# Zeroing a scratch table in seventeen pieces from the sync queue during the walk, and a neighbour comparison moved between the keys, in a graph network kernel

## What is computed

```
edge_index = jnp.stack([src, dst])
h = jnp.maximum(_layernorm(x, axis=-1), 0.0)
x = x + _L0_gnn_ref(h, edge_index, ...)
h = jnp.maximum(_layernorm(x, axis=-1), 0.0)
x = x + _L1_gnn_ref(h, edge_attr_8, edge_attr_64, edge_weight, ..., src, dst)
h = jnp.maximum(_layernorm(x, axis=-1), 0.0)
x = x + _L2_gnn_ref(h, ..., src, dst)
h = jnp.maximum(_layernorm(x, axis=-1), 0.0)
x = x + _L3_gnn_ref(h, L3_gnn_attn_w, src, dst)
```

## Time and profile before

| | us |
|---|---|
| median of 3 runs | 5092.41 (5090.03 to 5094.08) |
| profiled execution, its own time | 5095.59 |
| its span in the profile | 5093.8 |
| busy in the span: PE / DVE / ACT / POOL | 3575.9 / 4055.2 / 2002.8 / 1387.6 |

### The profile page before, as it was taken

One profiled execution on the slowest core, in us unless ns is written; L12 is line 12 of the kernel. 1 busy time (PEld: TensorE's weight loads), 2 busy tenths in 40 slices (PEclk: granted clock), 3 DMA queues, 4 the chain that ended last, 5 costly groups with the idle time before them and its releaser, 6 DMA issues. The chain is left out here.

```text
span 5093.8 us, 64935 instructions
## 1 busy us (share of the span) xinstructions
PE 3575.9 (70%) x19959; PEld 1591.3 (31%) x19959; DVE 4055.2 (80%) x7913; ACT 2002.8 (39%) x3932; POOL 1387.6 (27%) x2065
## 2 busy tenths in 40 slices
PE   3555551025608999999999359999999998147156
PEld 1111111001104555545555124444444443112122
DVE  4999994368866777777777789999999998588798
ACT  2888870046503333333333123333333332046065
POOL 0000006700055555555555112222222222100000
PEclk8999995567758999999999679999999999579579
DMA  6333338975433444444444113333333332345444
GB/s 265 137 137 140 142 137 275 363 228 186 138 122 102 112 112 112 111 111 111 111 112 112 32 53 87 90 88 89 89 88 90 87 90 73 123 153 201 150 157 172
DMA packets 347749, 673.72 MB, mean 132 GB/s; under 512 B 69724, under 2 KB 250396, under 8 KB 334864
## 3 DMA queue, kind: packets, MB, share of 16 engines
q1 hardware_dynamic: 305280, 564.32, 34.4%
q0 software_dynamic: 39680, 78.78, 5.9%
q10 hardware_dynamic: 2448, 26.48, 1.2%
HBM read 398.85 MB, written 270.50 MB: 131 GB/s over the span
## 5 line engine op out<-in xcount | busy, mean ns | idle before, releaser
L659 POOL DMA_INDIRECT arena<-h_table,gidx x808 | 763.4, 945 | 545.0 <-DVE gidx L1575 339.2
L792 PE MATMUL banks<-arena,lw 128*65 128x512 f32 (+3 forms) x1050 | 460.8, 595 | 298.6 <-DVE lw L1485 172.1
L1712 DVE TENSOR_TENSOR arena<-banks,arena 128x512 f32<-128x512 f32 x808 | 519.4, 684 | 110.9 <-PE banks L933 102.9
L741 PE MATMUL banks<-arena 128*128 128x500 bf16 x1440 | 365.6, 375 | 302.0 <-ACT arena L1079 293.5
L1587 DVE TENSOR_TENSOR arena<-banks,arena 128x512 f32<-128x512 f32 x808 | 535.1, 683 | 26.3 <-PE banks L838 0.6
L1719 DVE TENSOR_TENSOR arena<-banks,arena 128x512 f32<-128x512 f32 x808 | 536.1, 685 | 0.2 <-PE banks L938 0.2
L684 POOL TENSOR_TENSOR arena<-arena 128x72 f32<-128x72 f32 (+1 forms) x808 | 216.4, 299 | 984.3 <-DMA arena<-xs_dump 984.1
L1327 DVE TENSOR_SCALAR arena<-arena 128x500 bf16<-128x500 f16 x1440 | 440.7, 445 | 0.2 <-issue 0.2
L844 PE MATMUL banks<-arena 128*64 128x256 f32 x3232 | 438.6, 392 | 0.0
L949 PE MATMUL banks<-arena 128*64 128x256 f32 x3232 | 437.9, 392 | 0.5 <-DVE arena L1721 0.5
L938 PE MATMUL banks<-arena 64*128 64x512 f32 x1616 | 435.3, 616 | 0.8 <-DVE arena L1719 0.8
(11 more groups left out here) (281 smaller groups left out, 6446.1 us busy)
## 6 DMA issues: line engine op xcount, KB each, us to landing
arena<-c_flat SPq DMA_DIRECT2D x75, 1562.5 KB, 7.0
slots<-arena SPq DMA_DIRECT2D x90, 1000.0 KB, 3.9
arena<-hs_dump SPq DMA_DIRECT2D x404, 128.0 KB
arena<-mask_rows SPq DMA_DIRECT2D x50, 781.2 KB, 4.3
arena<-in_edge_attr SPq DMA_DIRECT2D x202, 128.0 KB
arena<-placed SPq DMA_DIRECT2D x202, 128.0 KB
xs_dump<-arena SPq DMA_DIRECT2D x202, 128.0 KB
hs_dump<-arena SPq DMA_DIRECT2D x202, 128.0 KB, 2.4
```

Source lines behind the costliest of these rows:

```text
L659: pool.indirect_dma_start(out=xs[par][:, k * D:(k + 1) * D], out_offset=None, in_=h_table, in_offset=bass.IndirectOffsetOnAxis(ap=gidx[par ...
L741: last = pe.matmul(ps[4 + r % 2][:, 0:BW], row_hot[r][:, k * P:(k + 1) * P], col_hot[r][:, k * BW:(k + 1) * BW], start=k == 0, stop=k == K ...
L792: last = pe.matmul(ps[j][0:rows, 0:n], lw[par][:, 0:rows], ptile[par][:, j * COLS:j * COLS + n], start=isinstance(b, int) and b == 0, stop ...
L1712: V.tensor_tensor(dt_[j % 2], ps[3 + j % 2][:, :], xat[q], ALU.mult).then_inc(dt_sb, 1)
```

## The change

The seventeen writes of zeros leave ScalarE's queue. SP issues one of them after every second `flush`, the first after eight steps of the walk. The tile, the sizes and the semaphore stay. The comparison's four lines move behind VectorE's four reads `offset` and ahead of its four reads `col_key`. Below the edit, line numbers in the changed kernel differ by a few.

```diff
@@ -421,6 +421,10 @@
             for i in range(SL // 8):
                 for par in range(2):
                     flush(i * 2 + par, par)
+                lo = i * CROW
+                if lo < W * D:
+                    n = min(CROW, W * D - lo)
+                    sp.dma_start(placed_v[:, lo:lo + n], zeros[:, 0:n]).then_inc(placed_zeroed, 16)
 
             for i in range(-(-WN // WIDE)):
                 n = min(WIDE * WD, N - i * WIDE * WD)
@@ -1058,11 +1062,6 @@
                     n = min(COLS, N - j * COLS)
                     act.activation(ot[0:rows, j * COLS:j * COLS + n], ps[j][0:rows, 0:n], ACT.Copy).then_inc(ot_sb, 1)
 
-            act.wait_ge(setup_d, 2)
-            for lo in range(0, W * D, CROW):
-                n = min(CROW, W * D - lo)
-                act.dma_start(placed_v[:, lo:lo + n], zeros[:, 0:n]).then_inc(placed_zeroed, 16)
-
             act.wait_ge(left_go, 1)
 
             def distance(s, r):
@@ -1287,10 +1286,6 @@
             dve.wait_ge(consts, 16)
             ran(V.tensor_scalar(row0, nid[:, 0:1], float(SL), None, ALU.mult))
             ran(V.tensor_copy(out=sel[:, :, :], in_=cst[:, C_SEL:C_SEL + 4 * P].rearrange("p (j m) -> p j m", j=4)))
-            dve.wait_ge(loaded, 16 * 6)
-            ran(V.tensor_tensor(same_prev[:, :], dsti[:, :], dprev, ALU.is_equal))
-            ran(V.tensor_tensor(same_next[:, :], dsti[:, :], dnext, ALU.is_equal))
-            ran(V.tensor_copy(out=firstc[:, 0:1], in_=dsti[:, 0:1]))
             settle()
 
             dve.wait_ge(key_ps, 1)
@@ -1300,6 +1295,10 @@
             for k in range(KE):
                 dve.wait_ge(key_ps, 2 + k)
                 V.tensor_tensor(offset[:, k, :], ps[k][:, 0:SL], base20, ALU.subtract).then_inc(key_sb, 1)
+            dve.wait_ge(loaded, 16 * 6)
+            ran(V.tensor_tensor(same_prev[:, :], dsti[:, :], dprev, ALU.is_equal))
+            ran(V.tensor_tensor(same_next[:, :], dsti[:, :], dnext, ALU.is_equal))
+            ran(V.tensor_copy(out=firstc[:, 0:1], in_=dsti[:, 0:1]))
             for k in range(KE):
                 dve.wait_ge(key_ps, 6 + k)
                 ran(V.tensor_tensor(col_key[:, k, :], ps[4 + k][:, 0:SL], base20, ALU.subtract))
```

## The result

| | before | after |
|---|---|---|
| median, us | 5091.98 (5090.03 to 5094.08, 4 runs) | 5030.05 (5030.02 to 5030.63, 4 runs) |
| profiled execution, its own time | 5095.59 | 5030.07 |
| its span | 5093.8 | 5028.3 |

The changed kernel is 61.9 us faster. The ratio of their times is 0.9879, with a 95% interval of 0.9861 to 0.9896.

The account below looks back on a forecast made before the run. DVE's two long early waits, for the walk's loads and for `x`, both behind the zeros, were taken as the bound. 25.8 + 29.3 = 55.1 us off 5092.4 gave 5037.3 us, range 5030 to 5050.

Parts of the forecast that it names:

- R1: Start: no tail on two engines, loads drain at full rate; 7 us more gained, 5030.3 us in all; chance 0.07.
- Part (a): Start: walk's loads without the zeros; DVE's first mask at 13.5 us, not 39.33; worth 25.8 us.
- the pairs with zero packets: Start, before the change: on one engine, load packets alternate with large zero packets, 0.41 us a pair; 72 pairs take 30 us.
- The sign of some 24 packets per microsecond: Start, new profile: about 24 DMA packets per microsecond should go on until DVE's first mask at 13 to 15 us.
- R2: Start: scattered single numbers, not zeros, make the loads late; DVE still starts at 39.33; 5063.1 us; chance 0.05.
- Part (b): From DVE's first mask to the walk's first step: 29.8 us instead of 59.1; worth 29.3 us.
- The lower clock: TensorE's selections before the walk: a lower granted clock in the second half of their run would cost 0.7 us.
- Part (c): Before the walk: `loaded` is there at 28 us, needed by 30.9 to 31.8; hidden, about 4 us to spare.
- the 40 packets at 0.18 us: Late engine after 13 us: five loads of 8 rows ahead of `x`, 7.3 us in all.
- R3: Comparison's new place: `x` ends the wait, rows cost 0.083 us each, `loaded` near 44 us; 5049 us; chance 0.07.
- Part (d): In the walk: zeros between flushes cost nothing; a piece ends 6.2 us after its issue, next flush issued after 7.4.
- R4: Walk's shared queue: pieces over 8.4 us each stop DVE 17 times; at 13 us each, 78 us, so 5115; chance 0.03.

## Why the prediction was right

**The number.** 5037.3 us was forecast and 5030.05 measured. The range's lower bound of 5030 was taken from R1, whose 5030.3 is nearly what was measured, though its condition (no tail on two engines) did not hold: it needed the first mask at about 6.5 us, and it came at 13.38. That the result fell inside the range and not just outside is luck. That DVE's first step would come 55 us earlier, and for which reasons, is not; the later 5034.45 also lies within the narrower 5034 to 5046. (The bounds given for the terms and the spread add up to 5034 and 5049, not 5046.)

**The reading of the start held.** Part (a) put DVE's first mask at 13.5 us; it came at 13.38. The two terms in it, a tail of about 22 rows on each of two engines and the pairs with zero packets, are borne out from both sides: with the zeros out of the start the mask moved to 13.4, and without the tail it came at 7.7 with the change and at 8.0 without it. The 0.5 us until the semaphore is seen is a part of the term that no run shows by itself. The sign of some 24 packets per microsecond up to the mask can be read only from 5.5 to 6.5 us, where 24 of 50 packets are of 512 B or more; behind that the later loads mix in (106 packets from 11 to 12 us). The cut loads also make R1's condition true: R1 gave 36.3 us for the first step, and the cut loads gave 36.9. In the changed kernel itself R1 didn't hold. R2, by which the loads are late by themselves, falls with the mask at 13.38.

**Part (b), mask to first step: 29.8 us forecast, 29.0 measured.** The term that was mis-sized is the selection. I took 8.72 / 6 = 1.45 us for each from the earlier trace rows. In the new trace DVE's reads of them come 1.21 us apart (29.20 and 30.41, 34.05 and 35.26) where DVE waits for TensorE, and all twelve take 15.65 us, not 17.4. By an estimate from these rows a block has 1.1 to 1.5 us that come once and not for each selection (15.65 - 12 x 1.21 and 8.72 - 6 x 1.21). DVE's own chain behind the eighth selection (40.37 - 35.26 = 5.1 us) set the end, as said. The lower clock that could have cost 0.7 us didn't come: the granted clock is 1.00 (2.4 GHz) from 20 to 40 us, while TensorE works without a pause.

What the step missed is the share of the comparison's move. The text laid the chain out with the move and called its 2.0 us covered by the selections. It didn't ask whether they were covered in the old place too. They are, by the 3.29 us in which DVE waits for the first products: with zeros only, the same 29.0 us. The move is worth something only with the zeros in their old place, 3 to 5 us.

**Part (c), `loaded`: 28 us forecast, 21.9 measured with the zeros only.** In the changed kernel itself nothing waits for it, so its time can't be read there. The term that was mis-sized is that of the 40 packets at 0.18 us, counted from 13 us on: between 14 and 15 us 842 of the 865 packets are already small ones, so on most engines the five loads ahead of `x` had run beside the tail. What they cost on the two late engines isn't shown. The price of 0.018 us for a row of `x` was good, as 16 / 865 = 0.0185 us for each packet of that microsecond, the 23 larger ones counted in. DMA traffic from 14 to 15 us in the changed kernel:

```profile
DMA packets 865, 0.29 MB, mean 289 GB/s; under 512 B 842, under 2 KB 842, under 8 KB 865
```

So R3 is out. The error had no effect, since nothing waits before 30.9 us.

**Part (d), nothing in the walk: held.** 666.0 us before, 665.9 after, with 26.5 MB more moved in it. A piece was priced a little low: it was to be through 6.2 us after its issue and to leave the next flush a free queue, and it took 7.3 (up to 8.2), while that flush was issued 7.0 us behind it. The slowest of the 90 flushes landed in 6.3 us (5.0 before and in the change's second trace), still far from the time at which DVE needs the buffer. The point from which R4 decides lies between the sizes that were run: at one piece nothing waits, at three DVE waits 1.9 us (2.9 by the sum), at seventeen 54.2 us (54). That is the mechanism of R4 at sizes the change doesn't have. The rule of the Trainium skill that was weighed there ("DMA: Bandwidth & Descriptors", section "Issuing engines are not separate DMA queues") says that another issuing engine saves only the time of issuing. The run on ScalarE's queue agrees: it was 2.0 us above the change, within the spread of both.

**The sum** was 55.1 us, and the first step moved by 56.0. In the later group the total followed it, 56.5; in the first comparison it was 61.9, and the 5.9 us beyond the first step were in no term of the forecast. They are also most of what separates 5030.05 from 5037.3.

## What to carry to other kernels

A large write that nobody needs for long shouldn't be issued beside the first loads. In this kernel every small packet of a load then waited behind a large one (116 of each in 3 us), and the engines that had the longest list of small packets decided. Put such a write where the queue has idle time, in pieces short enough that the transfer behind each still lands before somebody waits for it; the room for a piece can be read from the trace beforehand, and between the sizes run here the wait grew by 3.9 us for each further piece of 1.60 MB. When two waits follow one another, ask of each what it would be worth with the other standing, and of a moved instruction whether its old place wouldn't hide it as well.

## What the runs showed that I had not expected

Cutting three loads of 74 rows into 64 and 10 took 5.7 us off the first wait, though it adds three issues (0.5 us each on SP). The issue of one transfer can hold its engine for long: SP stood for 54.8 us in the issue of a transfer of 13 KB (line 398) in the kernel before, for 62.6 us in the kernel before with cut loads, and for 9.8 us in the changed kernel. So all that SP would issue next came later. And the first two traces, with the same work behind the walk, differ there by 9.4 us, and those of the kernel before on two chips by some 200, so a gain of a few us in a total of 5,000 is better read at the place where it arises.
